# A row tile of 64 rows for each head of a pair, in one fused block of attention and feed-forward layer

## The chip, the cores and the metric

The kernel runs on one core of one Trainium2 chip. The metric is the device time of one execution in microseconds (us). The kernel before took 575.08 us, the median of 3 runs (574.99 to 575.38).

## What is computed

A gated block of cross attention and a feed-forward layer, in float32, over four batches of 1024 tokens of width 256, with 154 context tokens for each batch.

```python
x = x + tanh(g_xattn[0]) * xattn(layernorm(x), ctx, ctx, Wq, bq, Wk, bk, Wv, bv, Wo, bo)
x = x + tanh(g_ffn[0]) * ffn(layernorm(x), W1, b1, A1, B1, R1, W2, b2, A2, B2, R2)

# xattn: 16 heads of 16 dims; q and k are rotated by position (xpos), k scaled down, q up
attn = softmax(q @ k.T) @ v;  return attn @ Wo.T + bo
# ffn: mole(relu(mole(x, W1..)), W2..), with 3 LoRA experts of rank 8
# mole(x) = x @ W + b + 1/8 * sum_e gate_e(x) * (x @ A_e) @ B_e,  gate = softmax(x @ R)
```

## The kernel before

The program is written out engine by engine, with counting semaphores between the engines; nothing is reordered by a scheduler. The work goes in eight chunks of 512 tokens (two for a batch). Step c (function `step` on every engine) does the attention of chunk c, the output projection, layer norm 2 and first feed-forward layer of chunk c-1 (d in the code), and the second feed-forward layer of chunk c-2 (e). Even steps begin a new batch, and also lay out its keys and values. Steps 0 and 1 have no chunk for the later parts, and the last chunk is finished behind the last step.

Products that need accuracy are done with numbers split in a high and a low part (suffixes hi and lo), three products for one. The rotated queries of a chunk are computed with tokens along the free dimension, in `probs`, 128 partitions of 8 head pairs x 8 dims x 2; a row of `qT` is a dimension of a head pair, and there lie the high part twice and the low part once: 96 rows for two heads, then two rows (KS = 96, KS + 1) for the negative maxima of both heads. The rows come into `qT` by DMA: six DMAs of 256 KB, each from 128 partitions of `probs` to 16 partitions of `qT`, four on SyncE's queue (L276, L280) and two on ScalarE's (L457). The semaphore q_rows counts them. The keys `km` lie in the same rows, once with the second head's rows masked out and once with the first's; so a product over all rows gives one head's scores.

TensorE works on a step in this order: output tiles 0 and 1 of chunk e (`out_tile`), output projection of chunk d (`project_out`), tiles 2 and 3 of e, transposes of the normalised x of d, then 16 pairs of maxima products (`max_scores`, L1128: scores with tokens on partitions, of which VectorE takes maxima, L750), in turn with the router and first layer of d. The first maxima product waits for q_rows; all else of TensorE queues behind it. Then the maxima are transposed, and go by small DMAs of 8 KB (L289) into the maxima rows of `qT`. Then come ten score steps (`scores`, with keys on partitions): eight "main" ones of two heads each for the first 128 keys, and two "rest" ones, in which the 26 last keys of four heads at a time are gathered on 128 partitions by `kr`. ScalarE takes the exponentials (L547). The values (`values`) of four heads each follow in four groups: one product for the rest (L1213) and four column tiles (L1216). The banks psX 0 and 1 and psX 2 and 3 take the scores in turn, so score step i waits for exponential i-2. The next chunk's query projection (`project_q`, L1011) stands ahead of the last group of values.

VectorE turns the heads back (`head_blocks`, `head_norm`, `head_back`, `head_low`), makes the rotation's products (`q_products`, L675), the rotation (`q_turn`, L682), and the low parts (`q_low`, L688).

## Time and profile before

| | before |
|---|---|
| median of 3 runs | 575.08 us |
| the profiled execution's own time | 568.85 us |
| its span | 567.0 us |
| TensorE busy (matmuls) | 502.2 us, 89% |
| VectorE busy | 392.3 us, 69% |
| ScalarE busy | 216.5 us, 38% |
| mean granted TensorE clock | 0.956 |

The span is the stretch from the first to the last instruction in the profiled execution. PE is TensorE, PEld its weight loads, DVE VectorE, ACT ScalarE, POOL GpSimd, SP SyncE; SPq and ACTq are the DMA issues on SyncE's and ScalarE's queues. A busy share is an average over stages that have different limits, so what a part is worth is read from the waits in its own stretch. The granted clock is 1.0 at 2.4 GHz and 0.5 at 1.2 GHz.

### The profile page before, as it was taken

The page shows a single profiled execution, that of the slowest core. Times are in us where ns is not written, and L with a number is a line of the kernel's source. Part 1 is how long each engine was busy: PE and PEld are TensorE (multiplying, and loading weights), DVE is VectorE, ACT ScalarE, POOL GpSimd, SP SyncE. Part 2 cuts the span into 40 slices and gives each one's busy share as a digit, 9 for nine tenths or more (in the row PEclk, how much of TensorE's full clock was granted, in tenths as well). Part 3 has the DMA queues.
Part 4 walks back from the last instruction along what each step waited for, and adds up shares of the span by engine and source line. Part 5 has one row for each costly group of instructions (what it writes and reads, how often), then busy time and mean ns, then how long its engine had stood idle before and what let it go on. Part 6 is the DMA issues. An engine that isn't in the chain of part 4 may idle for free.

```text
span 567.0 us, 7820 instructions
## 1 busy us (share of the span) xinstructions
PE 502.2 (89%) x3032; PEld 372.0 (66%) x3032; DVE 392.3 (69%) x904; ACT 216.5 (38%) x357; POOL 64.4 (11%) x113
## 2 busy tenths in 40 slices
PE   2478865999989898999989898999989998989897
PEld 1345344855967387845967487855977487847787
DVE  4757475858879387958878487958888486934633
ACT  3233512463335613463325513453326513361330
POOL 2336002010110102010101002010201001010100
PEclk9955976999999999999999999999999999999999
DMA  8391044011702062112702061113602071110001
GB/s 296 51 223 39 1 89 61 2 50 56 94 0 76 7 118 27 40 49 62 88 0 77 25 105 21 39 50 69 82 1 76 1 97 15 43 36 2 1 37 38
DMA packets 13329, 31.86 MB, mean 56 GB/s; under 512 B 1732, under 2 KB 2572, under 8 KB 13164
## 3 DMA queue, kind: packets, MB, share of 16 engines
q1 hardware_dynamic: 6983, 14.63, 15.2%
q10 hardware_dynamic: 6309, 16.73, 11.0%
q8 instruction: 24, 0.39, 0.3%
q14 instruction: 13, 0.11, 0.1%
HBM read 14.31 MB, written 4.19 MB: 33 GB/s over the span
## 4 chain that ended last, share of the span: by engine, by line
PE 50%; DVE 28%; ACT 10%; DMA 5%; issue 4%; POOL 2%; SPq 0%; ACTq 0%; DVEq 0%; POOLq 0%
PE psF L1099 13%; PE psX L1128 6%; PE psX L1199 5%; ACT probs L547 4%; DMA qT<-probs 4%; DVE max_t L750 4%; DVE probs L675 4%; PE psO L1213 3%; PE psF L1145 3%; ACT xn L431 3%; PE psO L1216 3%; DVE ln_s L601 2%; PE psX L1028 2%; PE psF L1105 2%; DVE probs L682 2%
## 5 line engine op out<-in xcount | busy, mean ns | idle before, releaser
L750 DVE TENSOR_REDUCE max_t<-psX 128x4 fp32r<-128x616 f32 x128 | 99.2, 795 | 9.1 <-PE psX L1128 7.4
L547 ACT ACTIVATE probs<-psX 128x1024 f32<-128x1024 f32 x64 | 64.3, 1025 | 50.8 <-PE psX L1199 50.8
L1145 PE MATMUL psF<-w_hi,h_hi 128*128 128x284 f32 (+1 forms) x240 | 72.1, 300 | 0.0
L1128 PE MATMUL psX<-km,qT 96*128 96x308 f32 x256 | 64.9, 343 | 8.1 <-DMA qT<-probs 4.2
L1145 PE MATMUL psF<-w_lo,h_hi 128*128 128x284 f32 (+1 forms) x240 | 70.4, 293 | 0.0
L1145 PE MATMUL psF<-w_hi,h_lo 128*128 128x284 f32 (+1 forms) x240 | 70.2, 292 | 0.0
L1128 PEld LDWEIGHTS psX<-km,qT 96*128 96x128 f32 x256 | 48.1, 206 | 24.1 <-DVE max_t L750 9.7
L463 ACT ACTIVATE h_hi<-psF 128x512 fp32r<-128x512 f32 x59 | 34.3, 593 | 54.4 <-PE psF L1105 54.4
L1145 PEld LDWEIGHTS psF<-w_hi,h_hi 128*128 128x128 f32 x240 | 45.2, 188 | 4.9 <-issue 4.8
L1145 PEld LDWEIGHTS psF<-w_hi,h_lo 128*128 128x128 f32 x240 | 45.2, 188 | 0.1
L1099 PE MATMUL psF<-xT_lo,w_hi 128*128 128x512 f32 x118 | 45.2, 398 | 0.0
L1145 PEld LDWEIGHTS psF<-w_lo,h_hi 128*128 128x128 f32 x240 | 45.2, 188 | 0.0
L1199 PE MATMUL psX<-qT,km 98*128 98x512 f32 x128 | 42.6, 434 | 2.6 <-ACT probs L547 2.6
L743 DVE SCALAR_TENSOR_TENSOR h_lo<-psF,h_hi 128x512 fp32r<-128x512 f32 x59 | 40.3, 683 | 6.5 <-ACT h_hi L463 6.5
L335 POOL TENSOR_TENSOR x<-x,tab 128x256 f32<-128x256 f32 x32 | 22.4, 732 | 185.7 <-DMA x<-in_x_dram 185.7
L1099 PE MATMUL psF<-xT_hi,w_hi 128*128 128x512 f32 x118 | 39.8, 419 | 0.0
L1199 PEld LDWEIGHTS psX<-qT,km 98*128 98x128 f32 x128 | 20.1, 191 | 28.0 <-issue 13.0
L1099 PE MATMUL psF<-xT_hi,w_lo 128*128 128x512 f32 x118 | 36.8, 393 | 0.0
L321 POOL TENSOR_TENSOR ln_v<-ln_m,eps 128x4 f32<-128x4 f32 x16 | 3.2, 202 | 255.3 <-DVE ln_m L606 255.3
L376 ACT ACTIVATE zT<-psO 96x256 fp32r<-96x256 f32 (+1 forms) x24 | 10.8, 451 | 53.9 <-PE psO L1163 29.0
L431 ACT ACTIVATE xn<-x,ln_b,ln_r 128x256 f32<-128x256 f32 x32 | 16.6, 590 | 34.7 <-POOL ln_b L328 34.7
L776 DVE STREAM_TRANSPOSE heads_t<-psF 128x512 f32<-128x512 f32 x16 | 11.4, 713 | 26.4 <-PE psF L1216 26.4
(181 smaller groups left out, 931.6 us busy)
## 6 DMA issues: line engine op xcount, KB each, us to landing
qT<-probs SPq DMA_DIRECT2D x32, 256.0 KB, 9.9
qT<-probs ACTq DMA_DIRECT2D x16, 256.0 KB, 7.6
x<-in_x_dram ACTq DMA_DIRECT2D x8, 512.0 KB, 3.2
x_ln<-in_x_dram ACTq DMA_DIRECT2D x7, 512.0 KB, 3.4
out_dram<-x ACTq DMA_DIRECT2D x7, 512.0 KB, 3.1
turn<-in_turns_dram SPq DMA_DIRECT2D x2, 512.0 KB, 10.1
heads_t<-in_w_dram SPq DMA_DIRECT2D x1, 1024.0 KB, 8.2
heads_t<-in_w_dram SPq DMA_DIRECT2D x1, 994.0 KB, 14.1
```

Source lines behind the costliest of these rows:

```text
L335: ins = nc.gpsimd.tensor_tensor(x1[:, u, k], x1[:, u, k], bo_b, ALU.add)
L431: nc.scalar.activation(xn[:, k, :], src[:, k, :], ACT.Identity, bias=ln_b[:, which, k:k + 1], scale=ln_r[:, which, k:k + 1]).then_inc(done ...
L463: nc.scalar.activation(h_hi[:, m, :], hidden_bank(d, m), ACT.Relu).then_inc(w1_hi_s.sem, 1)
L547: nc.scalar.activation(dst, psX[:, 2 * (i % 2):2 * (i % 2) + 2, :], ACT.Exp).then_inc(sc_exp.sem, 1)
L675: V.scalar_tensor_tensor(out=dst[:, w, :], in0=psX[:, s, :], scalar=bq_c[:, s:s + 1], in1=turn[:, u, w ^ s, :], op0=ALU.add, op1=ALU.mult) ...
L743: V.scalar_tensor_tensor(out=h_lo[:, m, :], in0=hidden_bank(d, m), scalar=0.0, in1=h_hi[:, m, :].bitcast(F32), op0=ALU.max, op1=ALU.subtra ...
L750: V.tensor_reduce(max_t[:, k, half, :].rearrange("p (h g) -> p g h", h=2)[:, 2 * j:2 * j + 2, :], psX[:, 2 * j:2 * j + 2, 0:2 * S].rearran ...
L1099: mm(hidden_bank(d, m), w[:, f, P * m:P * m + P], a[:, f, :], start=n == 0, stop=False)
L1128: ins = mm(psX[:, g % 4, 0:2 * S], qT[0:KS, g, tokens(k)], km[0:KS, g, :, :].rearrange("p h s -> p (h s)"), start=True, stop=True)
L1145: ins = mm(out_bank(d, k)[:, cs], a[:, m, tokens(k)], w[:, m, cs], start=m == 0 and i == 0, stop=m == HT - 1 and i == 2)
L1199: ins = mm(o_ps, km[:, n // 2, j, 0:P], qT[:, n // 2, :], start=True, stop=True)
L1213: mm(pv_bank(g), vr_sb[:, g, :], probs_r[:, g, :], start=True, stop=False)
```

## The change

In `qT`, `km`, `kr` and `ks` each head of a pair now has 64 rows of its own: 48 for the split dimensions, one for the maxima (row 48 and row 112), and rows of zeros. Products of the two heads of a score step go over 49 rows each, one from row 0 and one from row 64 (row tiles of 64 x 128), into two different banks. A rest step gathers four heads in each half: eight products instead of four. The maxima products go over 112 rows instead of 96; the maxima row of the first head has to be zero for them, so a DMA writes zeros there in every step. The rows of queries come in twelve DMAs of 128 KB, each from 64 partitions of `probs` to 8 partitions of `qT`.

The rest product of a group of values (`values_rest`) is apart from the others, and stands between the score steps. Each part of the values now takes two score pairs and writes to two banks, so blocks 0 and 1 are complete together, and likewise 2 and 3. The query projection follows all values. On VectorE the last two head blocks come together, and ahead of the query products; ScalarE's high part of the heads comes ahead of that of the queries. Even steps project the values ahead of the key transposes. At the start VectorE clears five tiles and the zeros ahead of the first layer norm's statistics. The order of heads in Wv and Wo follows the new order.

```diff
-KS = 96
-KA = KS + 2
+HR = 64
+KM = 3 * D
+KX = HR + KM
...
-        qT = sb("qT", [KA, NG, CH], F32R)
+        qT = sb("qT", [P, NG, CH], F32R)
-        km = sb("km", [KA, NG, 2, S], F32R)
-        kr = sb("kr", [KA, NG, P], F32R)
-        ks = sb("ks", [P, 2, NG, KA], F32R)
+        km = sb("km", [P, NG, 2, S], F32R)
+        kr = sb("kr", [P, 2, 5 * P], F32R)
+        ks = sb("ks", [P, 2, NG, P], F32R)
+        zero = sb("zero", [NG, CH], F32R)
...
+        def q_dst(hh, t, s):
+            r = HR * hh + D * t + D // 2 * s
+            return qT[r:r + D // 2, :, :].bitcast(F32)
...
                 for s in range(2):
                     sp.wait_ge(q_hi.sem, q_hi.at(c, s + 1))
-                    sp.dma_start(qT[16 * s:16 * s + 16, :, :].bitcast(F32),
-                                 probs[:, 4 + s, :]).then_inc(q_rows.sem, 16)
+                    for hh in range(2):
+                        sp.dma_start(q_dst(hh, 0, s), probs[64 * hh:64 * hh + 64, 4 + s, :]).then_inc(q_rows.sem, 16)
+                sp.dma_start(qT[KM:KM + 1, :, :].bitcast(F32), zero[:, :].bitcast(F32)).then_inc(q_rows.sem, 16)
                 for s in range(2):
                     sp.wait_ge(q_lo.sem, q_lo.at(c, s + 1))
-                    sp.dma_start(qT[32 + 16 * s:48 + 16 * s, :, :].bitcast(F32),
-                                 probs[:, s, :]).then_inc(q_rows.sem, 16)
+                    for hh in range(2):
+                        sp.dma_start(q_dst(hh, 1, s), probs[64 * hh:64 * hh + 64, s, :]).then_inc(q_rows.sem, 16)
...
-                    act.dma_start(qT[64 + 16 * s:80 + 16 * s, :, :].bitcast(F32),
-                                  probs[:, 4 + s, :]).then_inc(q_rows.sem, 16)
+                    for hh in range(2):
+                        act.dma_start(q_dst(hh, 2, s), probs[64 * hh:64 * hh + 64, 4 + s, :]).then_inc(q_rows.sem, 16)
...
+                if kind == "rest":
+                    for k in range(4):
+                        for hh in range(2):
+                            rows = slice(HR * hh, HR * hh + KM + 1)
+                            ins = mm(psX[:, 2 * (i % 2) + hh, :], kr[rows, n // 2, P * k:P * k + P], qT[rows, 2 * n + k, :],
+                                     start=k == 0, stop=k == 3)
+                else:
+                    for hh in range(2):
+                        rows = slice(HR * hh, HR * hh + KM + 1)
+                        ins = mm(psX[:, 2 * (i % 2) + hh, :], km[rows, n // 2, hh, 0:P], qT[rows, n // 2, :],
+                                 start=True, stop=True)
...
-                    head_blocks(d, 3)
-                    head_norm(d, 1)
-                    q_low(c)
-                    head_back(d, 1)
-                    head_low(d, 1)
+                    head_blocks(d, 2)
+                    head_blocks(d, 3)
+                    head_norm(d, 1)
+                    head_back(d, 1)
+                    q_products(c, u)
+                    head_low(d, 1)
+                    q_turn(c)
+                    q_low(c)
...
+            V.memset(zero[:, :].bitcast(F32), 0.0)
+            V.memset(qT[32:64, :, :].bitcast(F32), 0.0).then_inc(const_v.sem, 1)
+            V.memset(ks[:, :, :, :].bitcast(F32), 0.0).then_inc(const_v.sem, 1)
+            V.memset(kr[:, :, :].bitcast(F32), 0.0).then_inc(const_v.sem, 1)
+            V.memset(v_sb[:, :, :], 0.0).then_inc(const_v.sem, 1)
+            V.memset(vr_sb[:, :, :], 0.0).then_inc(const_v.sem, 1)
```

In SyncE's queue between two steps: `split` is the tile with the maxima, `probs` the rotated queries, `zero` the zeros. Before:

```order
L289 DMA qT<-split 1x4x512 [waits maxT_s1]
L289 DMA qT<-split 1x4x512
L276 DMA qT<-probs 16x8x512 [waits q_hi] x2
L280 DMA qT<-probs 16x8x512 [waits q_lo] x2
L289 DMA qT<-split 1x4x512 [waits maxT_s0]
L289 DMA qT<-split 1x4x512
```

And now:

```order
L297 DMA qT<-split 1x4x512
L284 DMA qT<-probs 8x8x512 [waits q_hi]
L284 DMA qT<-probs 8x8x512
L284 DMA qT<-probs 8x8x512 [waits q_hi]
L284 DMA qT<-probs 8x8x512
L285 DMA qT<-zero 1x8x512
L289 DMA qT<-probs 8x8x512 [waits q_lo]
L289 DMA qT<-probs 8x8x512
L289 DMA qT<-probs 8x8x512 [waits q_lo]
L289 DMA qT<-probs 8x8x512
L297 DMA qT<-split 1x4x512 [waits maxT_s0]
```

The four DMAs of queries, with 16 partitions of `qT` each (16x8x512), have become eight with 8 each and one of zeros; ScalarE's two have become four.

On TensorE, the end of the score part of step 0 (`qT` and `km` are scores, `wq` the query projection, `probs` and `v_sb` values, `wo` the output projection). Before:

```order
L1199 MATMUL psX<-qT,km 128x512 [waits sc_exp]
L1199 MATMUL psX<-qT,km 128x512
L1011 MATMUL psX<-xT_hi,wq_hi 128x512 [waits xT_hi_v,xT_lo_s,xT_hi_a,sc_exp]
L1011 MATMUL psX<-xT_hi,wq_hi 128x512
L1011 MATMUL psX<-xT_lo,wq_hi 128x512 x2
L1011 MATMUL psX<-xT_hi,wq_lo 128x512 x2
L1011 MATMUL psX<-xT_hi,wq_hi 128x512 x2
L1011 MATMUL psX<-xT_lo,wq_hi 128x512 x2
L1011 MATMUL psX<-xT_hi,wq_lo 128x512 x2
L1213 MATMUL psF<-probs_r,vr_sb 128x512 [waits xT_lo_s,sc_exp]
L1216 MATMUL psF<-probs,v_sb 32x512 x4
L1028 MATMUL psX<-wo_hi,split 128x256 [waits o_hi,o_lo,wo_lo,q_prod]
```

And now:

```order
L1229 MATMUL psO<-probs,v_sb 32x512 [waits sc_exp]
L1229 MATMUL psF<-probs,v_sb 32x512
L1229 MATMUL psO<-probs,v_sb 32x512
L1229 MATMUL psF<-probs,v_sb 32x512
L1016 MATMUL psX<-xT_hi,wq_hi 128x512 [waits xT_lo_s,xT_hi_v,xT_hi_a]
L1016 MATMUL psX<-xT_hi,wq_hi 128x512
L1016 MATMUL psX<-xT_lo,wq_hi 128x512 x2
L1016 MATMUL psX<-xT_hi,wq_lo 128x512 x2
L1016 MATMUL psX<-xT_hi,wq_hi 128x512 x2
L1016 MATMUL psX<-xT_lo,wq_hi 128x512 x2
L1016 MATMUL psX<-xT_hi,wq_lo 128x512 x2
L1033 MATMUL psX<-wo_hi,split 128x256 [waits o_hi,o_lo,wo_lo,q_prod]
```

The projection's products (psX<-xT, wq) have moved behind the last values, and the values of the last two parts (psO and psF in turn) stand together.

On VectorE, behind the scores of an odd step (psO and psF to `heads_t` are head blocks, the products with `turn` those of the queries). Before:

```order
L675 SCALAR_TENSOR_TENSOR probs<-psX,tab,turn 128x512 [waits q_ps,turn_loaded]
L675 SCALAR_TENSOR_TENSOR probs<-psX,tab,turn 128x512
L675 SCALAR_TENSOR_TENSOR probs<-psX,tab,turn 128x512 [waits q_ps]
L675 SCALAR_TENSOR_TENSOR probs<-psX,tab,turn 128x512
L682 TENSOR_TENSOR probs<-probs 128x512 [waits q_prod]
L682 TENSOR_TENSOR probs<-probs 128x512
L776 STREAM_TRANSPOSE heads_t<-psF 128x512 [waits pv_ps]
L784 RECIPROCAL den<-heads_t 128x32 [waits pv_t]
L786 TENSOR_TENSOR heads_t<-heads_t,den 128x2x16x16 [waits den_inv]
L688 TENSOR_TENSOR probs<-probs 128x512 [waits q_hi] x2
L791 STREAM_TRANSPOSE heads_t<-heads_t 128x512 [waits o_norm]
L795 TENSOR_TENSOR split<-heads_t,split 128x512 [waits o_hi]
```

And now:

```order
L803 TENSOR_TENSOR split<-heads_t,split 128x512 [waits o_hi]
L784 STREAM_TRANSPOSE heads_t<-psO 128x512 [waits pv_ps]
L784 STREAM_TRANSPOSE heads_t<-psF 128x512 [waits pv_ps]
L792 RECIPROCAL den<-heads_t 128x32 [waits pv_t]
L794 TENSOR_TENSOR heads_t<-heads_t,den 128x2x16x16 [waits den_inv]
L799 STREAM_TRANSPOSE heads_t<-heads_t 128x512 [waits o_norm]
L683 SCALAR_TENSOR_TENSOR probs<-psX,tab,turn 128x512 [waits q_ps,turn_loaded]
L683 SCALAR_TENSOR_TENSOR probs<-psX,tab,turn 128x512
L683 SCALAR_TENSOR_TENSOR probs<-psX,tab,turn 128x512 [waits q_ps]
L683 SCALAR_TENSOR_TENSOR probs<-psX,tab,turn 128x512
L803 TENSOR_TENSOR split<-heads_t,split 128x512 [waits o_hi]
L690 TENSOR_TENSOR probs<-probs 128x512 [waits q_prod]
```

The two head blocks and their norm now stand ahead of the four query products; the rotation (probs<-probs, waits q_prod) comes behind all of them and the low part of the heads.

## Rows read from the trace of the kernel before

**Rows 1.** The page, parts 1 and 2.

```profile
span 567.0 us, 7820 instructions
...
PE 502.2 (89%) x3032; PEld 372.0 (66%) x3032; DVE 392.3 (69%) x904; ACT 216.5 (38%) x357; POOL 64.4 (11%) x113
...
PEclk9955976999999999999999999999999999999999
```

**Rows 2.** Timeline, TensorE: start, length, instruction, [idle before <- releaser].

```profile
307.68 0.50 PE L1196 MATMUL psX<-qT,kr 98*128 98x512 f32 x1 [0.34 <-DVE max_t L750]
...
312.39 1.13 PE L1213 MATMUL psO<-probs_r,vr_sb 128*128 128x512 f32 x2 [0.64 <-ACT probs L547]
...
320.19 0.74 PE L1199 MATMUL psX<-qT,km 98*128 98x512 f32 x2 [0.65 <-ACT probs L547]
...
323.73 0.62 PE L1011 MATMUL psX<-xT_hi,wq_hi 128*128 128x512 f32 x2
...
327.42 1.06 PE L1216 MATMUL psF<-probs,v_sb 128*32 128x512 f32 x8
...
328.41 0.40 PE L1145 MATMUL psF<-w_hi,h_hi 128*128 128x284 f32 x1
...
335.26 0.71 PE L1028 MATMUL psX<-wo_hi,split 128*128 128x256 f32 x4 [0.31 <-DVE split L795]
...
338.21 0.28 PE L1163 MATMUL psO<-ident_r,zs 128*96 128x128 f32 x2
...
346.11 0.45 PE L1128 MATMUL psX<-km,qT 96*128 96x308 f32 x2
...
347.48 0.65 PE L1069 MATMUL psF<-xT_hi,a_sb 128*32 128x128 f32 x16 [0.92 <-DVE xT_lo L666]
```

**Rows 3.** Timeline, VectorE, the same stretch.

```profile
326.11 2.72 DVE L675 SCALAR_TENSOR_TENSOR probs<-psX,tab,turn 128x512 f32<-128x512 f32 x4
...
328.87 1.29 DVE L682 TENSOR_TENSOR probs<-probs 128x512 f32<-128x512 f32 x2
...
330.08 0.71 DVE L776 STREAM_TRANSPOSE heads_t<-psF 128x512 f32<-128x512 f32 x1
```

**Rows 4.** Timeline, TensorE, the odd step's scores and the even step behind.

```profile
368.88 0.50 PE L1196 MATMUL psX<-qT,kr 98*128 98x512 f32 x1 [0.35 <-DVE max_t L750]
...
391.20 0.77 PE L1111 MATMUL psX<-ident_r,ks 128*98 128x128 f32 x8
...
413.13 0.65 PE L1069 MATMUL psF<-xT_hi,a_sb 128*32 128x128 f32 x16 [0.92 <-DVE xT_lo L666]
```

**Rows 5.** The page, part 6: DMA, count, KB each, us to landing.

```profile
qT<-probs SPq DMA_DIRECT2D x32, 256.0 KB, 9.9
...
x_ln<-in_x_dram ACTq DMA_DIRECT2D x7, 512.0 KB, 3.4
```

**Rows 6.** DMA view of 331 to 343.6 us, and of 311 to 313 us.

```profile
DMA packets 866, 1.60 MB, mean 127 GB/s; under 512 B 96, under 2 KB 96, under 8 KB 864
...
DMA packets 16, 0.02 MB, mean 8 GB/s; under 512 B 8, under 2 KB 8, under 8 KB 16
```

**Rows 7.** Windows: stretch, length, busy time of each engine, PEclk, DMA share, GB/s.

```profile
311.34:311.67 0.33, 0.33 (x2) 0.00 (x0) 0.17 (x1) 0.33 (x1) 0.33 (x1) 1.00 0.09 25
...
331.50:343.20 11.70, 11.39 (x90) 11.20 (x89) 9.72 (x33) 1.50 (x4) 1.63 (x4) 1.00 1.03 137
...
340.50:342.50 2.00, 2.00 (x18) 2.00 (x17) 1.75 (x11) 0.00 (x0) 1.32 (x3) 1.00 1.03 115
...
84.50:87.10 2.60, 0.00 (x0) 0.00 (x0) 2.52 (x11) 0.00 (x0) 0.00 (x0) 1.00 1.00 173
...
87.10:97.40 10.30, 6.48 (x47) 4.51 (x48) 4.08 (x18) 3.38 (x7) 3.20 (x8) 0.50 0.40 48
```

**Rows 8.** Chain of waits, step 1: start, length, what.

```profile
81.31 11.64 DMA qT<-probs
...
93.09 0.85 PE psX L1128 x2
```

**Rows 9.** Timeline, VectorE, the start.

```profile
4.12 1.41 DVE L601 BATCH_NORM_STATS2 ln_s<-x_ln 128x6 f32<-128x256 f32 x4 [1.77 <-DMA x_ln<-in_x_dram]
...
6.15 0.91 DVE L908 MEMSET kr<- 98x1024 f32 x1 [0.16 <-issue]
...
7.11 0.48 DVE L909 MEMSET v_sb<- 128x512 f32 x1
```

**Rows 10.** Chain of waits, the first rows of queries.

```profile
25.11 11.54 DMA qT<-probs
```

More of the change, by code:

```diff
@@ L492, in step @@
                     load(b + u, 1 - u, c + 1)
-                if second:
+                if not first:
                     heads_high(d, 1)
@@ L819, in step @@
                     q_products(c, u)
-                if not second:
+                if first:
                     q_turn(c)
-                if first:
                     keys_bias(b)
@@ L1207, in values @@
                     if first:
-                        pe.wait_ge(const_v.sem, 6)
+                        pe.wait_ge(const_v.sem, 7)
                 if g == 2:
                     pe.wait_ge(pv_t.sem, pv_t.at(c, 1))
-                if g % 2 and not last:
-                    pe.wait_ge(xT_lo_s.sem, xT_lo_s.at(c + 1, g // 2 + 1))
+                if g == 3 and not last:
+                    pe.wait_ge(xT_lo_s.sem, xT_lo_s.at(c + 1, 1))
                 mm(pv_bank(g), vr_sb[:, g, :], probs_r[:, g, :], start=True, stop=False)
-                for j in range(4):
-                    h = 4 * g + j
-                    ins = mm(pv_bank(g)[32 * j:32 * j + 32, :], v_sb[:, h, :], probs[:, h % 8, :], start=False, stop=True)
+            def values(c, part):
+                pe.wait_ge(sc_exp.sem, sc_exp.at(c, (3, 5, 8, 10)[part]))
+                for p in (2 * part, 2 * part + 1):
+                    for hh in range(2):
+                        g, j = 2 * (p // 4) + hh, (p + 2 * hh) % 4
+                        ins = mm(pv_bank(g)[32 * j:32 * j + 32, :], v_sb[:, 4 * g + j, :], probs[:, 2 * (p % 4) + hh, :],
+                                 start=False, stop=True)
                 ins.then_inc(pv_ps.sem, 1)
@@ L1227, in step @@
                 if u == 0:
-                    if not first:
+                    if first:
+                        key_transposes(b)
+                        project_v(b)
+                    else:
+                        project_v(b)
                         pe.wait_ge(pv_t.sem, pv_t.at(d, 3))
-                    key_transposes(b)
-                    project_v(b)
+                        key_transposes(b)
                 if full:
-                    pe.wait_ge(pv_t.sem, pv_t.at(d, 3))
+                    pe.wait_ge(pv_t.sem, pv_t.at(d, 2))
                     out_tile(e, 0)
@@ L1282, in step @@
                     max_scores(c, 15)
[L1283 to L1301 removed]
+                scores(c, 0)
@@ new lines, in step @@
+                max_transposed(c, 1, first)
+                scores(c, 1)
+                if last:
+                    pe.wait_ge(w1_hi_s.sem, w1_hi_s.at(d))
+                    pe.wait_ge(w1_lo_s.sem, w1_lo_s.at(d))
+                    out_tile(LAST - 1, 2, 0, 3)
+                else:
+                    if not first:
+                        pe.wait_ge(w1_lo_s.sem, w1_lo_s.at(d))
+                    transpose_x(c + 1, psF[:, 1:3, :], ln1_out, xT_ps)
+                scores(c, 2)
+                values_rest(c, 0, first, last)
@@ new lines, in step @@
+                scores(c, 3)
+                values_rest(c, 1, first, last)
+                scores(c, 4)
+                values(c, 0)
+                if u == 1 and not last:
+                    ctx_transposed(b + 1, ctx_sb)
+                scores(c, 5)
+                scores(c, 6)
+                values(c, 1)
+                scores(c, 7)
+                if u == 1 and not last:
+                    project_k(b + 1)
+                if last:
+                    out_tile(LAST - 1, 2, 3, 5)
@@ L1302, in step @@
+                scores(c, 8)
+                values_rest(c, 3, first, last)
+                scores(c, 9)
+                values_rest(c, 2, first, last)
+                values(c, 2)
+                if last:
+                    out_tile(LAST - 1, 2, 5, 8)
+                values(c, 3)
                 if not last:
-                    pe.wait_ge(sc_exp.sem, sc_exp.at(c, 9))
                     project_q(c + 1, False)
-                values(c, 3, first, last)
-            pe.wait_ge(const_v.sem, 1)
@@ L1391, in position_tables @@
     pos = (np.arange(P)[:, None] + P * np.arange(2)[None, :]).reshape(-1)
-    ck, sk = (np.repeat(t.reshape(P, 2, 2, 1, D // 2), 2, 3).reshape(P, -1) for t in cs(pos, True))
-    r = np.arange(P)
-    head = np.where(r < KS, (r % D) // (D // 2), r - KS)
+    ck, sk = (t.reshape(P, -1) for t in cs(pos, True))
+    head = np.arange(P) // HR
     mask = np.stack([(head == 0), (head == 1)], 1).astype(f)
```

147 lines of the change are left out of this document (58 added, 89 removed).

## Prediction

> **What bounds the kernel now.** I read the page first: TensorE is busy 89% of the span, VectorE 69%, ScalarE 38%, and the granted clock is full from about 100 us on [rows 1]. So a matmul saved on TensorE can show in the time, if its operands come in time. The eight chunks (steps) run into each other, and from the third on they repeat, an odd and an even one. Next the timeline of one such stretch: scores begin at 307.68, stall four times on the exponentials of ScalarE (two of the four are shown, 0.64 and 0.65), the next chunk's query projection runs at 323.73, the last values end at 328.41, the output projection begins at 335.26, the first maxima product of the next step comes at 346.11 and its router at 347.48, after the 0.92 us that wait for layer norm 2 [rows 2]. The router starts 39.8 us behind the first score product; from 368.88 to 413.13, with the keys of a new batch in between, it is 44.25 us [rows 4].
>
> What the page does not show as a bound is the transfer of the query rows, because it is hidden. It runs from 331.5 to 343.2, 11.7 us at a DMA share of 1.03, that is all sixteen engines, yet it moves only 137 GB/s [rows 7]. Maxima products need all rows (L1124) and come at 346.11: 2.9 us of slack. In step 1, where no out tiles fill TensorE, the chain goes through it: 11.64 us of DMA, then the maxima product at 93.09 [rows 8]. This transfer is the place where the forecast is decided.
>
> **Queries' transfers.** Before, six DMAs of 256 KB, each from 128 partitions to 16 rows of qT. After, twelve of 128 KB, each from 64 partitions to 8 rows, and one of 16 KB of zeros to a single row. Bytes are equal but for 1%; packets stay 2 KB. Two things set the speed, and both get worse.
>
> First, how many engines share one DMA. Each engine ends its part with a small packet. Over the six row transfers there are 96 packets under 512 B, 16 each; over two maxima transfers (four packets of 2 KB, to one partition) there are 8, four each [rows 6]. So a DMA with 16 rows at its narrow side uses 16 engines, one with 4 pieces uses 4; I take 8 for 8 rows. The rows would also allow 16, by the 64 partitions read; then an engine has 48 packets as before. The Trainium skill, "DMA: Bandwidth & Descriptors", section on why a DMA increments its semaphore by 16, decides for 8: the number of engines is the largest up to 16 that divides the slowest dimension of both sides, and they are the lowest-numbered ones. By that rule an engine has 96 packets, by the other reading 48.
>
> Second, how fast few partitions take data. The 8 KB to one partition took 0.33 us, 25 GB/s; a 256 KB transfer alone to 16 partitions runs at 115 GB/s [rows 7]; 512 KB to 128 partitions land in 3.4 us [rows 5]. Speed goes with the partitions written, at 4 to 5 times the single rate for 16. For 8 rows I take half of 115, hence about 2.3 us for 128 KB, the time that 256 KB take now. The Trainium skill, "SBUF — State Buffer", section on the DMA port swizzle, has four neighbouring partitions (and those 32 further) share a port: 16 rows reach four ports, 8 rows two, so that also with 16 engines each 128 KB would take what 256 KB take now.
>
> With 8 engines each handles 96 packets and one of zeros instead of 48. At today's 11.7 / 48 = 0.244 us a packet that is 23.6 us; since ScalarE's and SyncE's DMAs, one behind another, will more often write to different halves of the partitions I take 23. Bounds: 11.7, if bytes alone count; 12 x 2.3 = 27.6, if nothing overlaps.
>
> **Step by step, times from the first score product.** *Score part.* Sixteen main products per step become eight pairs. A 512-column product follows the last one by about 0.23 us; two on different row tiles can run together, as the four column tiles of the values do (eight instructions in 0.99 us, 327.42 to 328.41 [rows 2]). Saved 8 x 0.23 = 1.8. The rest products double in number, and in pairs cost the same. TensorE now changes its tiling 18 times instead of 8 per even step; a change costs 0.1 to 0.2 us (of that 0.99, two rounds of 0.43 are work), so +1.6. The rests of the values, 1.05 us each, now stand where it waited for exponentials: of stalls worth 2.4 us (idle and drained pipeline) I leave 0.4. Sum -2.2: query projection ends at 18.5, not 20.7. In the odd step only 1.1 us of stall stood, and the two new neighbours, context and key projection, add changes: 22.3 becomes 20.9, -1.4.
>
> *VectorE's order.* The products of the query rotation now stand behind head blocks 2 and 3, norm and turning back. Behind even scores: values end at 15.8, blocks two times 0.73, norm 1.04, back 0.71 to 19.2, products 2.72 [rows 3] to 21.9, head low part 0.6, rotation at 22.5; before it was at 328.87, 21.2. Behind odd scores the keys' bias and rotation end late, blocks begin at 18.9, rotation at 25.5.
>
> *Odd step (three of them).* Rows: first packet 2.65 us behind the rotation (331.5 against 328.87), so 22.5 + 2.65 + 23 = 48.15. TensorE would want them at 35.65: projection 18.5 + two out tiles 6.3 + output projection 2.95 (335.26 to 338.21) + 7.9 to the maxima (338.21 to 346.11) [rows 2]. It stands still 12.5 us. Router at 48.6 instead of 39.8: +8.8. Afterwards VectorE is ahead, which removes 0.6 us of small waits behind the router. But the clock drops: in step 1 it was still full from 84.5 to 87.1, with TensorE already idle, and half from 87.1 to 97.4 [rows 7], that is until 4.3 us after the products went on at 93.09 [rows 8]; at half speed this costs 2.1. Together +10.3 x 3 = 30.9.
>
> *Even step (three).* Rows at 25.5 + 2.7 + 23 = 51.2, router 51.7 against 44.25: +7.4, -0.6 + 2.1 = +8.9, x 3 = 26.7. Without the rows it would come at 43.4: VectorE, 1.3 us late with the keys, feeds the gates and layer norm 2 later, +0.6 hidden here.
>
> *Step 1.* The same sum, with 1.6 us more for the half clock in the first scores: 24.1 + 2.7 + 23 = 49.8 against 40.7 from the first score product to 93.09: +9.1; the low clock is there already.
>
> *Start.* Before, VectorE takes the layer norm statistics at 4.12 and does its clearing behind them, in the shadow of the chain [rows 9]. After, six clears stand ahead, with 512, 4096, 2048, 1280, 512 and 512 elements a partition. From 1024 in 0.91 and 512 in 0.48 us (0.84 ns an element) they take 8.2 us from 0.7 on, the identity's cast 0.2: statistics at 9.1, +5.0, and all that follows hangs on them up to the first rows. Those take 11.54 us today [rows 10], +11.3 more. Start +16.3.
>
> *End.* Last step's scores -1.0, its blocks 2 and 3 together +0.2: -0.8.
>
> Sum: 30.9 + 26.7 + 9.1 + 16.3 - 0.8 = +82 us. The profiled execution took 568.85 (span 567.0 and 1.85 around it), so 651 for its like; the median of the runs is 6.2 above that execution, so 575.1 + 82 = **657 us**.
>
> **Rivals.** *Bytes alone count* (rows still 11.7 us, whether with 8 engines or 16): odd router at 22.5 + 2.65 + 11.7 + 0.4 = 37.3 against 39.8, -2.5 x 3; even 43.4, -0.85 x 3; step 1 -2.2; start +5.0; end -0.8: -8, **567 us**, the other side. It decides while rows take under about 13 us in odd steps. For it speaks that the first DMA of each burst runs faster than the average and that something beyond partitions may limit the mix; against it 25 GB/s to one partition, 4 engines and 16. *Engines hinder each other less*: with 8 engines on alternating partitions a packet takes 0.16 us, rows 15.5 us: 7.5 us less at eight places, and no clock drop, **about 590**. *Row tiles do not run together*: mains serial again, rest products 16 instead of 8: 16 x 0.23 = 3.7 us more a step, 29 in all; part of the change then does not do what it says. With slow rows **686**, with fast ones 596.
>
> **Chances.** Forecast 0.73; bytes alone 0.11; less hindrance 0.08; row tiles one after another 0.08. One us of rows is worth 8 us, so rows of 19 to 28 us give the forecast its own range 620 to 700. For 8 in 10 I reach down to the third case: 585 to 700; 567 stays out. A measurement here tells 0.2%, 1.2 us, from no change: faster 0.13, same 0.02, slower 0.85.
>
> **What would show it.** DMA share near 0.5 over about 23 us in each step (8 of 16 engines); 8 small packets per 128 KB; landing of queries' DMAs at twice 9.9 us; TensorE waiting for them at each step's first maxima product, about 12 us in odd and 10 in even steps; PEclk at half behind each; paired score products starting within some ns; statistics at 9 us. I am wrong if rows land within 13 us of the first packet, whatever the rest does; or if TensorE waits there and the clock stays full (13 us less).

## The result, and the profile after

The changed kernel takes 679.41 us (median of 4 runs, 678.94 to 681.52) against 575.04 for the kernel before: ratio 1.188, 95% interval 1.182 to 1.195, slower by 104 us. Its profiled execution took 679.29 (span 677.5). The forecast of 657 lay 22 us below; the profiled spans, 677.5 against 567.0, differ by 110.5 where the sum said 82.

The page after, parts 1 and 2 (busy time, share, instructions; then 40 slices), answers to [rows 1]:

```profile
span 677.5 us, 7990 instructions
PE 512.6 (76%) x3096; PEld 374.3 (55%) x3096; DVE 396.7 (59%) x907; ACT 216.1 (32%) x353; POOL 63.8 (9%) x113
...
PE   0633973299957997399948995599939995599897
...
PEclk9965596599997999599988998699978999599999
DMA  7194004301250105201250115120350105210000
```

TensorE's busy share fell from 89% to 76%; PEclk, which before stayed at 9 from about 100 us on, now dips once in each step. The view of waits (engine, tile, line waited for; us in total, times, longest) names the reason:

```profile
PE psX L1133 <- DMA qT<-probs: 113.5, 8, 19.1
```

There are eight waits for the query rows, one a step. Now the timeline of TensorE (start, length, instruction, [idle before <- releaser]) for the scores of chunk 3 and the even step behind them, which answer to [rows 4], and the scores of chunk 4 (380.56) with the odd step behind, which answer to [rows 2]:

```profile
304.84 1.20 PE L1201 MATMUL psX<-qT,kr 49*128 49x512 f32 x8 [0.34 <-DVE max_t L758]
...
325.23 0.62 PE L1016 MATMUL psX<-xT_hi,wq_lo 128*128 128x512 f32 x2
...
358.01 0.85 PE L1133 MATMUL psX<-km,qT 112*128 112x308 f32 x2 [10.45 <-DMA qT<-probs]
...
358.80 1.08 PE L1074 MATMUL psF<-xT_hi,a_sb 128*32 128x128 f32 x16
...
380.56 0.73 PE L1201 MATMUL psX<-qT,kr 49*128 49x512 f32 x4 [0.34 <-DVE max_t L758]
...
431.24 0.85 PE L1133 MATMUL psX<-km,qT 112*128 112x308 f32 x2 [13.91 <-DMA qT<-probs]
```

The last query projection starts at 325.23 and the key projection follows at 325.69, 20.85 us behind the first score product, as forecast (20.9). Then it stands still for 10.45 us before the first maxima product, and the router comes at 358.80, 54.0 us behind the score product (before 44.25). In the odd step it stands still for 13.91, up to 431.24, 50.7 us behind the score product. The windows (stretch, length, busy time of the engines, PEclk, DMA share, GB/s), against [rows 7], show what it waits for, and the clock behind the wait of the odd step:

```profile
332.60:357.20 24.60, 14.27 (x109) 13.38 (x107) 13.49 (x53) 5.85 (x14) 3.25 (x8) 0.87 0.52 66
...
431.20:435.20 4.00, 3.96 (x39) 3.15 (x40) 0.65 (x3) 0.19 (x1) 0.00 (x0) 0.50 0.00 0
...
435.20:454.60 19.40, 18.90 (x94) 15.28 (x93) 16.76 (x30) 7.78 (x16) 0.00 (x0) 0.97 0.07 29
```

Half of the DMA engines are busy for 25 us and move 66 GB/s, where all of them moved 137. In the 4 us behind the wait the granted clock is half (1.2 of 2.4 GHz). The DMA view of the same stretch, against [rows 6]:

```profile
DMA packets 882, 1.62 MB, mean 65 GB/s; under 512 B 103, under 2 KB 103, under 8 KB 879
```

There are 103 small packets beside thirteen transfers, so 8 each and not 16. VectorE's start (timeline), against [rows 9]:

```profile
2.26 3.47 DVE L905 MEMSET qT<- 32x4096 f32 x1 [0.89 <-issue]
...
6.22 1.76 DVE L906 MEMSET ks<- 128x2048 f32 x1 [0.49 <-issue]
...
8.20 1.12 DVE L907 MEMSET kr<- 128x1280 f32 x1 [0.21 <-issue]
...
10.40 1.39 DVE L609 BATCH_NORM_STATS2 ln_s<-x_ln 128x6 f32<-128x256 f32 x4
```

Statistics begin at 10.40, not 4.12; between two clears stand gaps of 0.2 to 0.9 us ("issue").

Split by the first score product of each chunk, which the timeline gives, the two traces compare as follows (us):

| stretch | before | after | measured | forecast |
|---|---|---|---|---|
| start to chunk 0's first score product | 52.41 | 75.33 | +22.9 | +16.3 |
| step 1 | 62.77 | 78.19 | +15.4 | +9.1 |
| steps 2, 4, 6 (even) | 65.6 each | 76.86, 75.72, 77.69 | +33.3 | +26.7 |
| steps 3, 5, 7 (odd) | 61.2 each | 74.46, 74.07, 75.22 | +40.2 | +30.9 |
| from the last one to the end | 71.3 | 70.0 | -1.4 | -0.8 |

### The profile page after: what moved, and what is told of

It reads as the page before. It is cut to its first block, busy times and chain, and to the rows that moved or that the text cites. A ratio compares the mean times of both kernels' runs of the same rounds, so it can differ in the third digit from the quotient of the medians.

```text
span 677.5 us, 7990 instructions
## 1 busy us (share of the span) xinstructions
PE 512.6 (76%) x3096; PEld 374.3 (55%) x3096; DVE 396.7 (59%) x907; ACT 216.1 (32%) x353; POOL 63.8 (9%) x113
## 4 chain that ended last, share of the span: by engine, by line
PE 43%; DMA 24%; DVE 18%; SPq 8%; issue 3%; ACT 3%; POOL 1%; DVEq 0%; POOLq 0%; ACTq 0%
DMA qT<-probs 24%; PE psF L1104 12%; PE psX L1133 7%; SPq L284 5%; PE psX L1206 3%; DVE probs L683 3%; DVE max_t L758 3%; PE psO L1229 3%; SPq L289 2%; PE psO L1221 2%; DVE heads_t L784 2%; PE psF L1221 2%; PE psF L1074 2%; PE psF L1150 2%; PE psF L1110 2%
## 5 line engine op out<-in xcount | busy, mean ns | idle before, releaser
L1133 PE MATMUL psX<-km,qT 112*128 112x308 f32 x256 | 69.2, 362 | 117.0 <-DMA qT<-probs 113.5
L1133 PEld LDWEIGHTS psX<-km,qT 112*128 112x128 f32 x256 | 50.6, 218 | 135.1 <-issue 118.5
L811 DVE STREAM_TRANSPOSE zc<-psF 128x128 f32<-128x128 f32 x7 | 2.2, 317 | 93.5 <-PE psF L1074 93.5
L1104 PE MATMUL psF<-xT_lo,w_hi 128*128 128x512 f32 x118 | 46.6, 411 | 0.0
L784 DVE STREAM_TRANSPOSE heads_t<-psO 128x512 f32<-128x512 f32 x16 | 11.4, 716 | 41.6 <-PE psF L1229 41.6
L1206 PE MATMUL psX<-qT,km 49*128 49x512 f32 x128 | 32.0, 495 | 1.5 <-ACT probs L555 1.5
L1229 PE MATMUL psO<-probs,v_sb 128*32 128x512 f32 x128 | 32.5, 602 | 0.0
L1229 PE MATMUL psF<-probs,v_sb 128*32 128x512 f32 x128 | 32.4, 602 | 0.0
```

The source lines that it names most:

```text
L784: V.transpose(heads_t[:, g, :, :].rearrange("p c r -> p (c r)"), pv_bank(g)).then_inc(pv_t.sem, 1)
L1104: mm(hidden_bank(d, m), w[:, f, P * m:P * m + P], a[:, f, :], start=n == 0, stop=False)
L1133: ins = mm(psX[:, g % 4, 0:2 * S].rearrange("p (h s) -> p h s", h=2), qT[0:KX, g, tokens(k)], km[0:KX, g, :, 0:S], start=True, stop=True)
L1206: ins = mm(psX[:, 2 * (i % 2) + hh, :], km[rows, n // 2, hh, 0:P], qT[rows, n // 2, :], start=True, stop=True)
L1229: ins = mm(pv_bank(g)[32 * j:32 * j + 32, :], v_sb[:, 4 * g + j, :], probs[:, 2 * (p % 4) + hh, :], start=False, stop=True)
```

## The experiments

Each was timed beside the kernel before, whose medians in these rounds were 570.2 to 572.7. "Rows" is the time from the first to the last 2 KB packet of a step's query rows, mean over steps 2 to 7, from the DMA packets of the trace: 11.5 us in the kernel before, 25.5 in the changed one. In the diffs the casts (`.bitcast`), the semaphores and their counts are left out.

**The cut of the transfers alone.** In the kernel before:

```diff
-sp.dma_start(qT[16 * s:16 * s + 16, :, :], probs[:, 4 + s, :])
+for hh in range(2):
+    sp.dma_start(qT[16 * s + 8 * hh:16 * s + 8 * hh + 8, :, :], probs[64 * hh:64 * hh + 64, 4 + s, :])
```

and likewise for the other two parts.

> The kernel before, with nothing changed but its six query-row transfers of a step: each is cut in two, 64 partitions to 8 neighbouring rows of qT (128 KB) instead of 128 to 16 (256 KB). If the cut of the transfers alone makes the loss (my theory), the rows of a step take about 25 us instead of 11.6, TensorE waits some 10 us at each step's first maxima product, and the time is about 660 (650 to 680). If the loss comes from the rest of the change (the order on VectorE, the clears at the start, the row tiles), the rows stay near 12 us and the time within 575 to 580. If a DMA costs by its number and not by its shape, twelve instead of six make 1 to 3 us more a step, and the time is 580 to 595.

Measured 640.3, ratio 1.120 (1.113 to 1.127), rows 22.1. Nothing but the shape and the number of the transfers changed, and it costs 70 us. (That it is not the number, a kernel with twelve fast ones shows below.) Expected were 25 us of rows and 650 to 680; that both are less is explained below, where the two queues are taken apart.

The view of waits:

```profile
PE psX L1131 <- DMA qT<-probs: 68.9, 8, 16.3
```

And the window over one step's rows:

```profile
309.20:331.30 22.10, 17.46 (x140) 16.75 (x132) 16.29 (x58) 6.70 (x16) 3.25 (x8) 1.00 0.51 72
```

**The rest without the transfers.** In the changed kernel each query-row transfer moves group 0 alone (`qT[r:r + 8, 0:1, :]` from 8 partitions).

> The changed kernel, with each of the twelve query-row transfers of a step moving group 0 alone (8 packets of 2 KB instead of 64; the other groups of queries stay zero, so this part of the scores is left out; qT is cleared over all its partitions at the start). It takes the transfers' duration away and keeps everything else. My theory (the transfers are the loss, the rest is worth a few us either way): rows in 3 to 4 us, no wait of TensorE for them from the third step on, clock full from 100 us, time 555 to 568. The rival, that the rest of the change loses too (VectorE's products behind the last head blocks, tiling changes), expects 580 or more.

Measured 562.8, ratio 0.985 (0.979 to 0.991); rows 6.0 us, not 3 to 4: in step 4 SyncE needs from 331.54 to 338.32 to issue its nine transfers, about 0.75 us each. In steps 2 to 7 the first maxima product comes 4.8 us or more behind the last packet, so TensorE doesn't wait for them. The rest of the change gains 7.8 us, and it does so although its statistics still begin late. The 104 us are the transfers', which also use up this gain.

**Engines or neighbours?** A head's 64 rows are put in another order, row 8i + j for feature i of part j, first with twelve transfers of 8 rows (half of the engines), then with six of 16 rows:

```diff
-r = HR * hh + D * t + D // 2 * s
-return qT[r:r + D // 2, :, :]
+return qT[HR * hh + 2 * t + s:HR * (hh + 1):8, :, :]   # twelve transfers
+return qT[2 * t + s:P:8, :, :]                         # six, source probs[:, s, :]
```

> The changed kernel with another order of the 64 rows of a head: feature i of part j stands in row 8i + j (j: queries' or keys' high and low parts and halves, 0 to 5; 6 the maximum; 7 unused). So each of the twelve transfers still goes from 64 partitions to 8 rows, but to rows 8 apart, spread over the 64 partitions of a head, instead of 8 neighbours. Products and all else are the same but for the keys' split (two copies instead of one). If the number of DMA engines that share a transfer is the limit (8 of 16, still so here), rows stay at 24 to 26 us and the time at 670 to 685. If it is how many neighbouring partitions take the data, rows fall to 12 to 15 us and the time to 565 to 590. If both count half, rows 18 us, time about 620.

> The same row order as in the spread kernel with twelve transfers, but each pair of transfers is one: from 128 partitions to 16 rows that stand 8 apart over all 128 partitions, six transfers of 256 KB a step and one of 32 KB of zeros. Sixteen engines and widely spread rows. If the number of engines is the limit, rows take 11 to 13 us and the time is 562 to 575. If the neighbouring partitions are the limit, the rows are as fast as in the kernel with twelve, 8 to 12 us, time 555 to 570. If neither is (the number of DMAs, the two queues), rows stay above 20 us and the time above 640.

With twelve: 576.1, ratio 1.008 (1.005 to 1.012), rows 12.0. With six: 559.7, ratio 0.980 (0.976 to 0.984), rows 7.5. The windows over one step's rows of the two, each from its own trace:

```profile
341.40:353.10 11.70, 10.94 (x85) 10.24 (x84) 7.45 (x34) 3.14 (x7) 3.25 (x8) 1.00 0.47 139
```

```profile
330.60:338.10 7.50, 7.50 (x63) 7.50 (x61) 6.59 (x28) 0.59 (x2) 1.54 (x4) 1.00 0.88 216
```

The first line holds the answer: the share is 0.47, still half of the engines, yet they move 139 GB/s, not 66. In this step a 2 KB packet takes 108 ns on average, and 256 ns in the same step of the changed kernel. What is read, the number of transfers and the engines are the same, so neither eight engines nor twelve transfers were the limit; eight neighbouring rows were. With the neighbours gone the engines do count: 12.0 with half of them, 7.5 with all. The kernel with six also has fewer transfers and writes each to both heads. The next experiment spreads the rows of eight engines further, too. The number of transfers is not taken apart from the engines; that the eight engines are busy nearly all the time (0.47 of at most 0.50) speaks for the engines.

**How far apart?**

```diff
+j = HR * hh + 32 * (t // 2) + (2 * t + s) % 4
+return qT[j:j + 29:4, :, :]                            # rows 4 apart in a block of 32
```

> The changed kernel with feature i of part j in row 4i + (j mod 4) + 32 (j div 4) of its head's 64 rows. Twelve transfers from 64 partitions to 8 rows as in the changed kernel and still half of the engines, but the 8 rows stand 4 apart in a block of 32, where the kernel with rows 8 apart took 11.7 us for the rows of a step and 576.1 us in all. The map of ports that the Trainium skill gives (SBUF, State Buffer, section on the DMA port swizzle) makes this 8 ports a transfer where 8 apart makes 4 and 8 neighbours make 2. If ports set the speed here (about 45 to 50 us times ports so far: 25.5 with 2, 11.7 with 4), rows take 6 to 8 us and the time is 558 to 566. If the 8 engines are what is left as the limit at 8 rows, rows stay at 11 to 12 us and the time at 572 to 580. If distance between rows is what counts and ports are not it, 4 apart is slower than 8 apart: over 12 us, over 577.

Measured 574.7, ratio 1.007 (1.004 to 1.010), rows 11.2. The window over one step's rows, with a share of 0.46:

```profile
341.90:353.40 11.50, 10.93 (x85) 10.24 (x84) 7.49 (x34) 3.14 (x7) 3.26 (x8) 1.00 0.46 142
```

By the map named in the expectation these are twice the ports of the twelve transfers 8 apart, and nothing is gained but 0.8 us: the second reading of this expectation, half of the engines as the limit from here on, holds. The third, that distance itself counts, does not: 4 apart is not slower.

**Do the two queues hinder each other?** In the changed kernel ScalarE's queue and SyncE's write to rows 32 to 47 and 0 to 15 of a head at one time.

```diff
-r = HR * hh + D * t + D // 2 * s
+r = HR * hh + D * (0, 2, 1)[t] + D // 2 * s            # keys' parts in the same order
```

> The changed kernel with one edit: the queries' rows for the keys' low part, which ScalarE's queue writes, stand in rows 16 to 31 of a head instead of 32 to 47, and the low parts of the queries in 32 to 47. Each transfer is as before (64 partitions, 8 neighbouring rows). In the changed kernel both queues write at one time to rows 0 to 15 and 32 to 47, which by that map are the same ports; here they write to different ones. If two transfers to the same ports hinder each other, rows fall from 25.5 us to 20 to 22.5 (the kernel before with halved transfers, whose two queues wrote to different ports, took 22), and the time to 645 to 660. If each transfer is limited by itself (two ports, eight engines), rows stay at 25 to 26 us and the time at 675 to 685.

Measured 652.6, ratio 1.144 (1.138 to 1.150), rows 21.9, waits 86.3 us instead of 113.5. The window over one step's rows:

```profile
321.10:342.40 21.30, 14.24 (x108) 13.35 (x107) 13.45 (x53) 5.85 (x14) 3.26 (x8) 0.96 0.51 76
```

The view of waits:

```profile
PE psX L1133 <- DMA qT<-probs: 86.3, 8, 16.4
```

This one edit of which rows stand where is worth 27 us. It fits the first experiment: there ScalarE's queue wrote to rows 64 to 95 and SyncE's to rows 0 to 63, and the rows took 22.1. The Trainium skill ("SBUF — State Buffer", section on the DMA port swizzle) gives a map in which four neighbouring partitions share a port, the four 32 further share it too, and those 64 further don't. The measured rows agree with it: 8 neighbours (two ports) are half as fast as 16 (four), and two queues hinder each other on rows 0 and 32 of a head, much less on rows that the map puts on other ports. The ports themselves are seen in no trace here.

**The fast transfer in the kernel before.**

```diff
-sp.dma_start(qT[16 * s:16 * s + 16, :, :], probs[:, 4 + s, :])
+sp.dma_start(qT[s:KS:6, :, :], probs[:, 4 + s, :])
```

and likewise the other two parts from rows 2 + s and 4 + s.

> The kernel before with one edit: each of its six query-row transfers writes its 16 rows 6 apart (rows j, j + 6, ..., j + 90 of qT) instead of 16 neighbours. Bytes, packets, engines and all other instructions are the same (keys keep the old row order, so the scores are not those of the reference). If the spread of the rows alone makes the transfer fast, rows take 7 to 8 us instead of 11.6. Since TensorE waited for the rows only at the start and in step 1, only these two places gain, 3.5 to 4.5 us each: 561 to 564 against 570.2 to 570.6, and what the kernel with late clears gains beyond that (555.2) belongs to the other parts of the change. If the other steps were held by the rows as well, through something that the waits don't show, each gains too: 555 or less. If 6 apart doesn't spread enough, no change, 570.

Measured 573.0, ratio 0.9995 (0.9965 to 1.0025): no change. The rows fall to 6.7 us, as the window over those of one step shows:

```profile
331.30:338.00 6.70, 6.38 (x52) 6.19 (x51) 5.17 (x16) 0.84 (x2) 0.00 (x0) 1.00 0.98 235
```

None of the three readings of the expectation holds: the rows did get fast, and the time stayed. At the start the first maxima product comes at 35.06 instead of 36.78, now behind 1.44 us of waiting for VectorE (`vr_sb`, L697), so 1.7 us are gained and not 3.5 to 4.5. In step 1 it comes at 90.85 instead of 93.09, but the router behind it gains only 0.8 us, as the timelines show, first of the kernel before, then of this one:

```profile
93.87 1.08 PE L1069 MATMUL psF<-xT_hi,a_sb 128*32 128x128 f32 x16
```

```profile
90.85 0.86 PE L1128 MATMUL psX<-km,qT 96*128 96x308 f32 x2
93.05 1.08 PE L1069 MATMUL psF<-xT_hi,a_sb 128*32 128x128 f32 x16 [1.33 <-ACT xT_hi L376]
```

With the rows in time TensorE waits 1.33 us for ScalarE's high part of the normalised x (`xT_hi`): a second wait stood right behind the one for the rows. The granted clock is then half for 4.9 us behind the router (until 97.91) and for 3.5 us before (until 97.38), and the next chunk's first score product is at 115.00 against 115.18. In the other steps the transfer was hidden, as forecast; the last chunk's first score product comes 0.24 us earlier than before (495.44 against 495.68). Behind it this execution takes 75.7 us to the end and that of the kernel before 71.3; in this one the clock is at half from 531.4 to 538.2 us, a drop that the other does not show and that the transfer is not seen to cause. So the kernel with late clears, which comes next, does not owe its gain to a fast transfer alone.

**The clears at the start.** On the kernel with six spread transfers:

```diff
-V.memset(zero, 0.0); V.memset(qT, 0.0); V.memset(ks, 0.0); ...   # ahead of ln1_stats(0)
+V.memset(kr, 0.0); V.memset(v_sb, 0.0); ...                      # behind it
+nc.gpsimd.memset(qT[:, 0:4, :], 0.0)                             # and [:, 4:8] behind the first rstd
```

> The kernel with rows 8 apart in six transfers (559.7 us), and the clears at the start taken from in front of the layer norm statistics: VectorE clears kr, v_sb, vr_sb, zero and ks behind them, GpSimd clears qT in two halves between its constants. If the clears were a cost only because the statistics stood behind them (they begin at 10.2 in the kernel that this is made from, at 4.1 in the kernel before), the statistics begin at 4 to 5, the first score product comes 5 to 6.5 us earlier, and the time is 553 to 555. If the clears then delay the next thing on their engines (the split of x on VectorE, the first reciprocal root on GpSimd), 1 to 3 us of it are left: 556 to 558. No theory expects over 560.

Measured 555.2, ratio 0.972 (0.967 to 0.977), 4.5 us less than its parent, just above the 553 to 555 that were expected. VectorE's timeline:

```profile
3.93 1.41 DVE L611 BATCH_NORM_STATS2 ln_s<-x_ln 128x6 f32<-128x256 f32 x4
...
5.97 1.12 DVE L911 MEMSET kr<- 128x1280 f32 x1 [0.21 <-issue]
...
9.63 1.76 DVE L917 MEMSET ks<- 128x2048 f32 x1 [0.38 <-issue]
...
12.46 0.69 DVE L667 CAST xT_hi<-psF 128x512 fp32r<-128x512 f32 x1 [1.07 <-PE psF L983]
```

Statistics begin at 3.93, the split of x at 12.46 (12.96 in the kernel before, 18.46 in the parent) and so not late, and chunk 0's first score product comes at 51.71 instead of 57.77, 6.1 us earlier. The profiled spans differ by the same 6.1 (553.0 against 559.1); the medians by less, and the runs of this kernel alone spread by 2.1 us.

**The row tiles undone** for the sixteen main products:

```diff
-rows = slice(HR * hh, HR * (hh + 1))
-ins = mm(psX[...], km[rows, n // 2, hh, 0:P], qT[rows, n // 2, :])
+ins = mm(psX[...], km[:, n // 2, hh, 0:P], qT[:, n // 2, :])
```

> As the kernel with late clears, but the sixteen main score products of a step use all 128 rows of the array, one after another (the keys of the other head are zero there), instead of eight pairs of row tiles; the rests stay in pairs. By the prediction's terms: 8 x 0.23 = 1.8 us more a step on TensorE for the pairs, less 8 or so tiling changes of 0.1 to 0.2, so +0.2 to +1.0 us a step if TensorE sets the end there: 555 to 562 against 553.5 of its parent. If the pairs did not run together at all it is 3 to 8 us faster than its parent. If the score part waits for ScalarE's exponentials anyway, within 1 us of it.

Measured 553.8, ratio 0.971 (0.965 to 0.977): the same as its parent within the spread, 0.2 us a step less in the trace. The groups of TensorE (busy time, mean ns of one | idle before), of the parent and of this kernel:

```profile
L1209 PE MATMUL psX<-qT,km 64*128 64x512 f32 x128 | 31.4, 487 | 1.5 <-ACT probs L557 1.5
```

```profile
L1208 PE MATMUL psX<-qT,km 128*128 128x512 f32 x128 | 51.4, 488 | 0.0
```

The pairs do run together: both products of a pair start within 0.01 us. The 20.0 us less of busy time (2.5 a step) are no price for that, since in this kernel products that start behind a rest of the values are counted while they wait for it (from 302.23 below). By their starts, full-array products follow each other after 0.23 us (308.63, 308.86 and 309.09), so a pair saves 0.23 and eight save the forecast 1.8. The timeline shows where it goes, first of the parent, then of this kernel:

```profile
302.89 0.50 PE L1209 MATMUL psX<-qT,km 64*128 64x512 f32 x2
...
303.33 1.12 PE L1224 MATMUL psO<-probs_r,vr_sb 128*128 128x512 f32 x2
...
304.38 0.50 PE L1209 MATMUL psX<-qT,km 64*128 64x512 f32 x2
...
304.81 1.13 PE L1224 MATMUL psF<-probs_r,vr_sb 128*128 128x512 f32 x2
```

```profile
301.23 0.70 PE L1208 MATMUL psX<-qT,km 128*128 128x512 f32 x2
...
301.77 1.02 PE L1223 MATMUL psO<-probs_r,vr_sb 128*128 128x512 f32 x2
...
302.23 1.02 PE L1208 MATMUL psX<-qT,km 128*128 128x512 f32 x2
...
303.09 0.59 PE L1223 MATMUL psF<-probs_r,vr_sb 128*128 128x512 f32 x1
```

One round of a rest of the values (two full-array products) and a pair takes 1.48 us (303.33 to 304.81), one of a rest and two full products 1.32 (301.77 to 303.09). The pair saves 0.23 and the round is 0.16 longer, so its two changes of tiling cost 0.39, about 0.2 each, the upper end of the forecast 0.1 to 0.2. That is why the expected +0.2 to +1.0 us a step came out as -0.2.

**The low clock behind the wait.** The changed kernel with products added inside the waits of steps 2 to 7:

```diff
+for n in range(50 if u else 36):        # second run: 62 and 46
+    mm(psX[:, 0, :], w1_hi[:, 0, 0:P], w1_hi[:, 1, 0:CH], start=True, stop=True)
 max_scores(c, 0)
```

> The changed kernel with added work: before the first maxima product of steps 2 to 7 TensorE runs 36 (even) or 50 (odd steps) 512-column products whose result is overwritten, about 8 and 11 us by 0.227 us each, inside waits for the rows of 10.5 to 11.3 and 13.9 to 15.1 us. Nothing is shortened but the idle time, so what falls is the cost of the low clock behind the wait. By the prediction's term (2.1 us a step) it gains 12 us or so: 664 to 670. If the low clock costs nothing because VectorE sets the pace behind the wait, 676 to 681. If the added products end too late for a step's rows, it is slower than 680.

Its four times spread from 672.9 to 684.2 (median 677.8 where 664 to 670 were expected; ratio 1.180, 1.170 to 1.189), which settles nothing against 1.188. The trace, of the slowest of the four, shows the expected effect missing: 2.4 to 3.9 us of each wait stayed idle, and the clock behind it was half nevertheless (window behind the wait of step 4, of which 2.42 us were idle).

```profile
360.00:364.00 4.00, 3.53 (x39) 2.68 (x39) 0.65 (x3) 0.00 (x0) 0.00 (x0) 0.57 0.00 0
```

> The changed kernel with the same added products as the shorter filler, now 46 (even) and 62 (odd steps), 10.4 and 14.1 us, so that under 1.1 us of each wait for the rows stays idle; with 36 and 50 of them 2.4 us stayed idle and the granted clock still fell to half right behind the wait (0.57 over the next 4 us). If the low clock behind the wait costs what the comparison with the kernel that doesn't wait gives (1.0 to 1.9 us a step, 9.3 over six steps; the prediction's term was 2.1 gross), the clock stays full behind the waits of steps 2 to 7, router to next score product takes 21.5 us instead of 22.5 to 23.5, and the time is 667 to 672. If VectorE sets the pace there whatever TensorE's clock is, router to score product stays over 22.3 us and the time at 677 to 682.

Measured 671.0, ratio 1.173 (1.165 to 1.182): with more work it is 8.4 us faster than the changed kernel, as expected (667 to 672). Of each wait 0.3 to 1.2 us stay idle. The timeline of TensorE in step 4:

```profile
352.83 0.55 PE L1133 MATMUL psX<-km,qT 112*128 112x308 f32 x2 [0.32 <-DMA qT<-probs]
...
374.01 1.20 PE L1201 MATMUL psX<-qT,kr 49*128 49x512 f32 x8 [0.34 <-DVE max_t L758]
```

And the window right behind that wait:

```profile
353.00:357.00 4.00, 4.00 (x48) 3.17 (x49) 1.60 (x8) 0.48 (x2) 0.00 (x0) 1.00 0.01 4
```

The clock stays at 1.00, and from the first maxima product to the next score product it takes 21.2 us in each step, against 22.5 to 23.5 (mean 23.1) in the changed kernel: 1.9 us a step for the half clock. The last chunk's first score product comes 12.7 us earlier (594.88 against 607.54); 4.3 of them are lost behind it, where this execution, as that of the kernel before with fast rows, has the clock at half for a while (from 629.5 to 636.3).

## Why the prediction was right, and where it missed

*Bound.* This was right: TensorE and the hidden transfer behind it. The transfer had 2.9 us of slack and became 14 us longer.

*Queries' transfers.* The time per step was forecast at 23 and is 25.5; the bounds of 11.7 and 27.6 hold it. Of its two reasons the first is refuted: eight engines with 97 packets of 0.244 us each give 23.6 only because a packet's 0.244 us were themselves made by neighbouring rows (in the kernel before with rows 6 apart, and all else as it was, a packet takes 0.13). With the same eight engines and rows 8 apart a packet takes 0.108 us and the rows 12.0. That this reason gave nearly the number of the other is luck. The second reason, few neighbouring rows at half the rate of 16, is the one that acts. The step that made the number too small is the discount from 27.6 to 23, given because the DMAs of ScalarE and SyncE would more often write to different halves of the partitions. What mattered was not the half but the place in it: the two queues wrote rows 32 apart within a head, and moving one part by 16 rows gives 21.9. This is 2.5 us a step. In step 1 rows take 25.9, at the start 28.4, where the weights load beside them (no run here keeps the weights away).

*Score part.* The query projection's end was forecast at 18.5 us behind even scores and at 20.9 behind odd ones, and measured at 18.4 (398.98) and 20.85. Pairs save the 1.8 a step; a change of tiling costs 0.2, the upper end of the forecast, so that the row tiles of the main products gain nothing (-0.2 us a step without them).

*VectorE's order.* The rotation was forecast 22.5 and 25.5 behind the first score product, measured 22.0 and 25.0 (329.86 against 304.84).

*Odd and even steps.* The waits were forecast at 12.5 and about 10 and are 13.9 to 15.1 and 10.5 to 11.4. The misses are 3.1 and 2.2 us a step. The rows are 2.5 of each. From the last packet to the router the sum allowed 0.45, and it took 1.5 to 2.1 (0.7 to 1.3 to the maxima product and 0.8 more): 1.0 to 1.4 more. Against that the rows began 0.45 us earlier than forecast, and the stretch behind the router was 0.4 (odd) and 0.8 us (even) shorter. The clock's 2.1 is 1.9.

*Step 1.* It is +15.4 instead of +9.1: the rows 2.9 more than forecast, the rotation at 25.95 instead of 24.1, and 1.3 us from the last packet to the product, for which the sum had nothing.

*Start.* It is +22.9 instead of +16.3: the statistics were 6.3 us late, not 5.0, since the sum of the clears left out the gaps between them (the clears take 7.8 us, less than the 8.2 of the sum, and the gaps 1.6), and the rows took 28.4, not 23.

*Rest of the change, end.* The rival with fast rows was -8 in all; with few bytes it is -7.8. The term of the end, -0.8, measured -1.4. With rows of 7.4 and late clears the trace gives -3.0 for each odd step (forecast -2.5), -0.4 for each even one (-0.85) and -3.3 for step 1 (-2.2).

*The sum against the median.* It is made from an execution of 568.85, 6.2 under the median of before. The spans differ by 110.5, the medians by 104.4; the profiled changed kernel is at its own median, so the 6.2 us that the forecast carried over from one to the other were not there, and the forecast missed the median by 22 and not 28 us by luck. Against the profile the forecast was 651 and the miss 28 us: 18 from the rows of seven steps, 5 from the first rows, 1.3 from the clears, and the rest from the last packet to the product and the late rotation of step 1.

## What to carry to other kernels

A transfer between partitions was priced here by which partitions are written at one time, over all queues, before its bytes and its engines: 8 neighbouring rows were more than twice as slow as the same 8 rows at a distance of 8, and the order of rows in a contraction is free. A transfer that is hidden by 3 us is a bound in waiting: write down its slack before a layout change. Here the layout with 64 rows for each head pays (553.8 to 555.2 us, 2.8% under the kernel before) as soon as each part's rows stand 8 apart, are written by one transfer over both heads, and the clears go behind the statistics. Which of the reorderings in the change brings the gain no run separates; the row tiles of the main products do not, nor does a fast transfer in the kernel before.

Where a wait is taken away, look at the next one behind it before its length is booked as a gain: in step 1 of the kernel before, faster rows brought the first maxima product 2.2 us forward and the router behind it 0.8.

## What the hardware showed that I had not expected

- A packet of 2 KB inside the memory of the core took, on average in step 4, 108 ns (8 rows 8 apart), 131 (16 rows 8 apart), 218 and 256 (8 neighbours, the two queues apart and together). A packet's duration is no constant to multiply with.
- The clock fell behind waits of which only the last 2.4 to 3.9 us were idle (0.57 over 4 us behind 2.4), and stayed full behind 0.3 to 1.2 us. Products with no use made the kernel 8.4 us faster.
- Row tiles that halve the time of two products gave nothing where full-array work stands between them: 1.48 us for a round with a pair, 1.32 for one with two full products.
